# A 128 x 512 block of activations is transposed by VectorE instead of TensorE, in a decoder layer for one Trainium2 core

## The reference, cut to what matters

```
x = layernorm(x + self_attention(x))            # this result is called x1
x = layernorm(x + cross_attention(x, ctx))      # ctx has 1601 rows a batch; this result is x2
x = layernorm(x + ffn(x))                       # base projection + one of 8 adapters, chosen by a loss
```

## Time and profile before

| | us |
|---|---|
| median of 3 runs | 1649.25 |
| lowest and highest | 1646.03, 1655.02 |
| the profiled execution | 1650.58 |
| its span | 1648.8 |
| TensorE busy | 1586.7 (96%) |
| VectorE busy | 1238.2 (75%) |
| ScalarE busy | 1053.2 (64%) |
| GpSimd busy | 161.2 (10%) |

### The profile page before, as it was taken

One profiled execution on the slowest core, in us unless ns is written; L12 is line 12 of the kernel. 1 busy time (PEld: TensorE's weight loads), 2 busy tenths in 40 slices (PEclk: granted clock), 3 DMA queues, 4 the chain that ended last, 5 costly groups with the idle time before them and its releaser, 6 DMA issues.

```text
span 1648.8 us, 25559 instructions
## 1 busy us (share of the span) xinstructions
PE 1586.7 (96%) x9632; PEld 588.7 (36%) x9632; DVE 1238.2 (75%) x1790; ACT 1053.2 (64%) x1998; POOL 161.2 (10%) x151
## 2 busy tenths in 40 slices
PE   6779999999999999999999999999999999999997
PEld 5442323332333333332333323433333323332233
DVE  5788777877788777887888777887778777887522
ACT  2227776676666666676666766676666776666661
POOL 7311000100011000100001000110001000000000
PEclk8899999999999999999999999999999999999999
DMA  5655071623517071442707163361707234150010
GB/s 156 116 143 101 25 138 41 101 69 86 96 40 127 28 131 40 90 93 62 116 22 134 32 113 69 69 112 52 121 12 122 61 52 77 50 78 5 11 33 16
DMA packets 118663, 125.22 MB, mean 76 GB/s; under 512 B 35186, under 2 KB 100339, under 8 KB 118540
## 3 DMA queue, kind: packets, MB, share of 16 engines
q1 hardware_dynamic: 117724, 123.06, 38.3%
q10 hardware_dynamic: 816, 0.53, 0.1%
HBM read 84.18 MB, written 35.03 MB: 72 GB/s over the span
## 4 chain that ended last, share of the span: by engine, by line
PE 85%; DVE 7%; ACT 3%; issue 3%; DMA 1%; SPq 0%; POOL 0%; POOLq 0%; DVEq 0%; ACTq 0%
PE banks L1122 23%; PE values L1141 23%; PE banks L1082 12%; PE work L1012 5%; PE work L998 5%; PE work L957 4%; DVE xneg_max_pieces L1439 4%; PE work L1019 3%; PE work L1025 3%; ACT xprobs L1260 3%; PE work L1004 2%; PE work L1028 1%; PE work L942 1%; PE work L1037 1%; DMA max_dram<-xneg_max_rows 1%
## 5 line engine op out<-in xcount | busy, mean ns | idle before, releaser
L1260 ACT ACTIVATE xprobs<-banks 128x512 f32<-128x512 f32 x1664 | 900.5, 595 | 408.3 <-PE banks L1122 405.0
L1439 DVE TENSOR_REDUCE xneg_max_pieces<-banks 128x2 f32<-128x1024 f32 x768 | 909.0, 1219 | 258.4 <-PE banks L1082 257.2
L1122 PE MATMUL banks<-xq_stacks,xk_stacks 99*128 99x512 bf16 (+1 forms) x1664 | 517.7, 385 | 9.9 <-ACT xprobs L1260 3.0
L1141 PE MATMUL values<-xprobs,xv_rows 128*17 128x512 f32 x3328 | 437.9, 598 | 1.3 <-ACT xprobs L1260 1.3
L1122 PEld LDWEIGHTS banks<-xq_stacks,xk_stacks 99*128 99x128 bf16 (+1 forms) x1664 | 127.4, 97 | 398.8 <-ACT xprobs L1260 273.2
L1082 PE MATMUL banks<-xk_stacks,xq_stacks 49*128 49x512 bf16 (+1 forms) x2048 | 250.3, 335 | 14.2 <-DVE xneg_max_pieces L1439 12.3
L1082 PEld LDWEIGHTS banks<-xk_stacks,xq_stacks 49*128 49x128 bf16 x2048 | 57.2, 94 | 327.6 <-DVE xneg_max_pieces L1439 212.9
L1510 POOL TENSOR_TENSOR xk_parts<-xk_rest,xk_parts 128x401 bf16<-128x401 f32 (+1 forms) x64 | 59.0, 923 | 660.5 <-ACT xk_parts L1239 660.5
L1141 PEld LDWEIGHTS values<-xprobs,xv_rows 128*17 128x17 f32 x3328 | 55.1, 95 | 122.9 <-issue 117.6
L1505 POOL TENSOR_TENSOR xrstd<-xrstd,mhalf 128x4 f32<-128x4 f32 x23 | 23.2, 1011 | 652.4 <-DVE xrstd L1314 652.4
L1012 PEld LDWEIGHTS work<-xvT,ctxT_a 128*128 128x128 f32 (+1 forms) x416 | 54.3, 192 | 13.6 <-issue 3.9
(11 more groups left out here) (295 smaller groups left out, 1007.3 us busy)
## 6 DMA issues: line engine op xcount, KB each, us to landing
xk_stacks<-key_parts_dram SPq DMA_DIRECT2D x186, 200.1 KB, 13.0
key_parts_dram<-xk_parts SPq DMA_DIRECT2D x144, 100.0 KB, 2.2
xq_stacks<-parts_dram SPq DMA_DIRECT2D x186, 64.0 KB, 8.8
ctxT_a<-in_ctxT SPq DMA_DIRECT2D x4, 1601.0 KB, 7.5
ctxT_b<-in_ctxT SPq DMA_DIRECT2D x4, 1601.0 KB, 7.5
parts_dram<-xq_parts SPq DMA_DIRECT2D x45, 128.0 KB, 2.0
key_parts_dram<-xk_parts SPq DMA_DIRECT2D x48, 100.2 KB, 5.2
xa<-in_x SPq DMA_DIRECT2D x8, 512.0 KB, 16.3
```

Source lines behind the costliest of these rows:

```text
L1122: pe.matmul(at, kst[0:ROWS[par], k, h2, par, t * P:(t + 1) * P], qst[0:ROWS[par], k, h2, par, :], start=True, stop=True).then_inc(made, 1)
L1141: last = pe.matmul(av[32 * j:32 * j + HD + 1, :], vals[:, k, t, gr * GH + j, :], probs[:, sl % 2, j, :], start=t == 0, stop=t == XKT - 1)
L1260: nc.scalar.activation(probs[:, sl % 2, j, :], score_bank(n)[0], ACT.Exp).then_inc(exped, 1)
L1439: nc.vector.tensor_reduce(nmp[:, of % 2, :, j2, q, piece], pairs[n % MRING][:, :, :], AX.X, ALU.max, negate=True).then_inc(on["mxr"], 1)
```

## The change

Three edits. The two x1T jobs leave `IN_BETWEEN`; in their stead VectorE has sixteen steps `turn`, each a transpose of one 32-token by 256-dim piece, written block by block to the 32 partitions where it belongs in `xT`: two steps in each of places 7 to 11, three in place 12, three in place 13. Each raises the semaphore `x1_turned`, for which qproj and the next load of `xa` wait. In `SLOT_END`, qproj 0 (places 12 and 13) and v 2 (places 14 and 15) change places. In `VECTOR_WORK` of place 5, the scaling of the last group goes ahead of the application of x1's norm.

```
         IN_BETWEEN = {
-            8: ("x1T", 0, NEXT), 11: ("x1T", 1, NEXT), 14: ("x2T", 0, PREV), 16: ("x2T", 1, PREV), 18: ("v", 3, NOW),
+            14: ("x2T", 0, PREV), 16: ("x2T", 1, PREV), 18: ("v", 3, NOW),
...
-            (("qproj", 0, NEXT), 2), (("v", 2, NOW), 2), (("enc", 0, PREV), 2), (("gram", 0, PREV), 2),
+            (("v", 2, NOW), 2), (("qproj", 0, NEXT), 2), (("enc", 0, PREV), 2), (("gram", 0, PREV), 2),
...
+        N_TURNS = (P // 32) ** 2
+        def turn_steps(first, last):
+            return [("turn", "x1", n, NEXT) for n in range(first, last)]
...
-            5: [*norm_steps("apply", "x1", 0, 2, NEXT), ("scale", "o", 3, PREV)],
-            6: norm_steps("apply", "x1", 2, 4, NEXT), 8: norm_steps("stats", "x2", 0, 2, PREV),
-            9: norm_steps("stats", "x2", 2, 4, PREV), 10: [("aggr", "x2", 0, PREV)],
-            11: norm_steps("apply", "x2", 0, 2, PREV), 12: norm_steps("apply", "x2", 2, 4, PREV),
+            5: [("scale", "o", 3, PREV), *norm_steps("apply", "x1", 0, 2, NEXT)],
+            6: norm_steps("apply", "x1", 2, 4, NEXT), 7: turn_steps(0, 2),
+            8: [*norm_steps("stats", "x2", 0, 2, PREV), *turn_steps(2, 4)],
+            9: [*norm_steps("stats", "x2", 2, 4, PREV), *turn_steps(4, 6)], 10: [("aggr", "x2", 0, PREV), *turn_steps(6, 8)],
+            11: [*norm_steps("apply", "x2", 0, 2, PREV), *turn_steps(8, 10)],
+            12: [*norm_steps("apply", "x2", 2, 4, PREV), *turn_steps(10, 13)], 13: turn_steps(13, N_TURNS),
...
             elif name == "qproj":
                 if part == 0 and not ph.first:
-                    pe.wait_ge(on["w_free"], ph.order.after(("x1T", 1, b)))
+                    pe.wait_ge(x1_turned, N_TURNS * b)
...
+            elif name == "turn":
+                a, c = divmod(q, P // 32)
+                if q == 0:
+                    v.wait_ge(on["normed"]["x1"], b)
+                v.transpose(xT[32 * c:32 * (c + 1), :, :].rearrange("p k (n a i) -> p a k n i", a=P // 32, i=32)[:, a],
+                            xa[32 * a:32 * (a + 1), :, :].rearrange("p n (k c i) -> p c k n i", k=CH, i=32)[:, c]
+                            ).then_inc(x1_turned, 1)
...
             if b > 1:
                 nc.sync.wait_ge(on["x1_out"], 16 * (b - 1))
-                nc.sync.wait_ge(on["w_free"], MAIN.order.after(("x1T", 1, b - 1)))
+                nc.sync.wait_ge(x1_turned, N_TURNS * (b - 1))
```

More of the change, by code:

```diff
@@ L789, in cross_attention_and_ffn @@
         scaled = sem("x_outputs_scaled")
+        x1_turned = sem("x_x1_turned")
         x1_in = sem("x_x1_in")
```

## The result

The changed kernel is slower: 1675.34 us median of 4 runs (1671.66 to 1677.62) against 1649.08 (1646.03 to 1655.02), ratio 1.0149 with a 95% interval of 1.0132 to 1.0166. That is +26 us where +6 was forecast, and outside the range (1642 to 1671). The profiled execution took 1671.66 us, its span is 1669.9 us (before: 1648.8). It is the fastest of the four; what the 3.7 us between it and the median are, no trace shows.

A forecast was written before the change was run, and what follows sets the result against it. PE bounds the kernel nearly everywhere; in places 5 to 14 DVE would become the bound, 34.4 against 33.2 us. Six batches of +1.2 less batch 0's 1.2 give +6.2 unrounded: 1650.6 + 6.2 = 1656.8 us, range 1642 to 1671.

The forecast's parts named there:

- What bounds the stretch: Places 5 to 14, batches 1 to 6: DVE becomes the bound at 34.4 us; PE's floor is 31.2, before 33.2.
- DVE's need of 29.7 us: DVE's busy time in places 5 to 14 before the change, leaving 3.5 us a batch unused of 33.2.
- I take T = 0.33 + 0.03 = 0.36 us.: Price T of one turn on DVE, start to start; thirteen ahead of x2T's wait take 4.7 us a batch.
- its sign of being wrong: In places 5 to 14: a turn shorter than 0.27 or longer than 0.45 us start to start, among other signs.
- Rival 2: fp32 turns take double time, T = 0.6 us: about +26 us, 1677 us; chance 0.13 at or above 0.5.
- halfway case: Turns on DVE don't overlap each other: 0.44 us each, +12 us, 1663 us.
- In batch 0 ... the turns fit: Batch 0 has 5.9 us of DVE room for 4.7 of turns, and both x1T jobs are saved: -1.2 us.
- The reordering removes 0.5 us: Scaling ahead of apply steps in place 5: place 6 takes 3.40 instead of 3.92 us, covered only by DVE's spare time.
- Edits with no price: Exchange of qproj and third v piece, qproj's wait for turns, later SP transfers, changed semaphore, unchanged GpSimd order: taken as nothing.
- Batch 7's 0: Batch 7 has no next x, so the change was forecast to cost 0 there.
- cheap turns that fit: Turns on DVE below break-even T = 0.27 us; at T = 0.13, -12 us, 1638.6 us; chance 0.17.
- late inverses: Inverses, behind query parts on SP's queue, come late for place 18's scaling: +21 us on top, 1678 us; chance 0.05.

The follow-up runs named there:

- Experiments 1 and 2: Changed kernel with one of sixteen turns left: 1639.14 us; changed kernel with six turns instead of thirteen ahead of x2T: 1650.62 us.
- experiment 4: Changed kernel with all sixteen turns reading and writing partitions 0 to 31 (not a true transpose): 1653.88 us against 1649.86 for the kernel before.
- Experiment 7: Kernel before with only the scaling moved ahead of the two apply steps in place 5: 1651.24 us against 1650.66.
- experiment 8: Kernel before with only qproj 0 and v 2 exchanged: 1652.63 us against 1649.86, ratio 1.0010.
- experiment 5: Changed kernel with all turns writing the first quarter but each reading another quarter than the one before: 1668.44 us against 1652.15 for the kernel before.
- experiment 3: Changed kernel with plain copies of the same shapes, tiles and partitions in place of the transposes: 1665.62 us, ratio 1.0084 to the kernel before.
- experiment 6: Changed kernel with the turns as plain copies that read and write only the first quarter: 1644.15 us against 1652.15 for the kernel before, one run.

## Why the prediction was wrong

- **What bounds the stretch: right.** 31.2 us of floor for PE, no gap once DVE is the bound, waits at the second max pair and ahead of x2T. Experiments 1 and 2 hit 31.2 and 33. DVE's need of 29.7 us was 0.5 too high (29.2 in experiment 4, without idle time), which hid as much of the error in T.
- **The step that failed: "I take T = 0.33 + 0.03 = 0.36 us."** The rows behind it, 0.33 us for a statistics step and 0.13 us for the short transpose, are of instructions that start on partition 0 for reading and writing, like their neighbours. The turns change the quarter at every step but the first. That takes the overlap of 0.08 to 0.1 us from the turn and from what stands in front of a group: 0.465 us, over the 0.45 that the prediction had named as its sign of being wrong, and 0.11 a group. In the stretch it is +3.1 us instead of +1.23: 6 x 1.9 = 11 us. The loop missed its forecast by 23.0 - 6.2 = 16.8 us; the rest is batch 0 (2.5), the clock in batch 6 (1.6), batch 7 (0.9) and what stands behind the stretch (0.6). With one quarter a turn does cost 0.34 us (experiment 4), so the extrapolation over the number of elements was good; its condition was not looked at. The trace of before had a hint: the scaling, which works on partitions 64 to 127, lasts 0.69 us from 698.14, and the next reduction starts at 698.86, after a gap of 0.03 us where others overlap, though it waits for nothing of the scaling (DVE's timeline of the kernel before):

```profile
698.86 2.36 DVE L1439 TENSOR_REDUCE xneg_max_pieces<-banks 128x2 f32<-128x1024 f32 x2
```

- A rule of the Trainium skill says this: *VectorE: DVE Perf Modes*, "Two Vector instructions with no wait between them", has an instruction held until every earlier one has finished when its input starts in another quadrant (32 partitions) than that of the last instruction that read the same memory, SBUF or PSUM, or its output in another than that of the last one that wrote it. The runs agree in both directions (0.465 with, 0.34 without, and either side alone suffices). The prediction drew on another section of that page, by which a turn takes 0.327 us, and not on this one.
- **Rival 2 had the size but not the cause.** It put T at 0.6 and the time at 1677 us for two passes over fp32; that the median came to 1675 is luck, since experiment 4 has 256 fp32 elements in 0.34 us, like the statistics. Its halfway case, turns that don't overlap each other, was priced 0.44 us and 1663 us; the gap of 0.03 us and the 0.11 us a group make 0.50 us of it.
- **"In batch 0 ... the turns fit": wrong by 1.5 us of the 2.5.** The count over a stretch (5.9 us of room for 4.7) says nothing of the last place: qproj's wait for the turns is exposed where no x2T stands ahead. 1.17 us in the row, 1.5 us in the place. The other 1.0 us stands in two places that differ from trace to trace.
- **"The reordering removes 0.5 us": right for place 6, and worth nothing,** as the prediction had it for a DVE that is the bound. Experiment 7 adds that even with DVE's idle time of before it is worth 0.1 us a batch.
- **Edits with no price:** 0.8 us in experiment 8's profile, not decided by its interval (0 to +3.5 us). Batch 7's 0 was 0.9, of which that profile has 0.6.
- Fallen rivals: cheap turns that fit (0.465 is over the 0.27 of break-even), and late inverses (no such wait appears).

## What to carry to other kernels

Before work moves from a bound engine to one with idle time, count that time in the very stretch, not over the span, and place the work where the idle is: with the sixteen turns in places 7 to 13 the kernel took 1.5% more, with fifteen of them in places 14 to 21, and other jobs moved to suit, 0.5% less. And price a small instruction by rows that share not only its size but its partitions: here a VectorE piece of 256 elements that started in another quarter than the one before it cost its full length and a gap of 0.03 us (0.465 us instead of 0.34), and the instruction ahead lost its overlap too (0.11 us).

## What the runs showed of the hardware that was not expected

PE stood still for 1.75 us ahead of x2T in six batches. Behind one of them, in batch 6, the granted clock fell to its lower level (1.2 GHz): its mean is 0.59 over the 4 us from 1313, and the two qproj matmuls took 1.92 us there, 1.02 us in batch 3 (736.73). Timeline of PE, and the stretch with the granted clock behind POOL's column:

```profile
1314.06 1.92 PE L1012 MATMUL work<-xT,xqT 128*128 128x512 f32 x2
...
1313.00:1317.00 4.00, 4.00 (x14) 1.24 (x14) 2.92 (x4) 1.92 (x6) 0.00 (x0) 0.59 0.00 0
```

That cost 1.6 us once. In experiment 5 two of six such stops were followed by it, in the kernel before, with no such stop in this part of the loop, none: a stop of PE can cost more than its length, in some batches and not in others.

In experiment 3 the two copies of place 11 took 1.40 us in batches 1 to 5 (1.41 in batch 3, from 726.13), where two copies in other places took 0.60; each time a GpSimd subtraction of 0.96 us started within 0.01 us of them (726.12). That is 0.8 us of the stretch. In experiment 6 the copies started 0.08 us ahead of the same subtraction (337.54 and 337.62) and took 0.48 us, and the subtraction took 1.22. In the changed kernel two transposes started with it (726.81 and 726.80) and took 0.90 us, as elsewhere. A copy of this kind (256 elements in 0.30 us, where a statistics step lasts 0.41) and GpSimd's subtraction thus seem to wait for each other; it was not tested by itself, and the transposes show nothing like it.
